# Selective-scan layers: one injection in three on GpSimd, du on VectorE, the B row copied earlier on ScalarE

## The chip, the cores and the metric

The kernel runs on one core of a Trainium2 chip. The metric is the device time of one execution in microseconds (us), from runs of the same program; the profile is of one further execution, with its own time beside it. A core has five engines that the text names as the profile does: PE (TensorE), DVE (VectorE), ACT (ScalarE), POOL (GpSimd) and SP (SyncE, which here only issues DMAs).

## The reference, cut to what matters

Four residual layers work on x of shape (4, 32, 32, 96). Each is `x = x + layer(groupnorm(x))`. Layers 0 and 3 (the "cross" layers) are four-direction selective scans over the 1024 pixels of an image; layer 1 is a small feature layer and layer 2 a scan in one direction. For a cross layer, per image and direction:

```
delta = softplus(dts + bias)              # (192 channels, 1024 pixels)
h[t]  = exp(delta[t]*A)*h[t-1] + delta[t]*u[t]*B[t]     # for each of 16 states
y[t]  = sum over states of h[t]*C[t], plus u[t]*D
```

The four directions' y are summed, normalised over the channels, gated by silu(z) and projected back to 96 channels.

## The kernel before

`cross_scan_layer` is one hand-written program for all engines; every wait is a semaphore wait in the code, and each engine runs its instructions in the written order. A **turn** is one image in one pixel order (rows or columns); there are 4 images x 2 orders = 8 turns in each of the two cross layers, 16 in all. The orders are r = 0 and r = 1. A turn has 16 **groups** of 3 **tiles** (c = 0, 1, 2): 48 tiles of 128 x 1024 float32. The 16 groups are 2 scan directions d times 8 pairs of states p; the three tiles c of a group are three blocks of 64 channels, with two states of each over the 128 partitions.

For each tile the engines do this, with the lines of the kernel before:

- ACT, `turn_of` (L777): decay = exp(delta*A) into one of three SBUF buffers. At c = 1 it first runs `copy_b` (L767): the group's B row, which a DMA has spread over 128 partitions in SBUF (`b_rows`), is copied to one of two PSUM tiles `b_ps`.
- DVE, `inject_tile` (L916): the **injection** du*B, from du in SBUF and the B row in PSUM, into PSUM. Then the **scan** (L931): state = decay*state + injection, along the pixels.
- POOL (L841): the **read**, state*C, from SBUF to SBUF.
- PE (L651): y accumulated in PSUM over the tiles by four matmul instructions.

So the chain of a tile is ACT and DVE, then POOL, then PE. Rings hold it together: a scan waits until the read three tiles back is done (three `state` buffers), a read until the y two tiles back is done (two `read` buffers).

Beside this, the turn does **side work**: it finishes the image before (z, shift, cent, var, out; in r = 0 turns except the first image's) and prepares the next turn's u, B and C, delta and du. The tables FINISH and PREPARE give the tile at which PE issues each half of a side matmul into the only side bank, `side_ps`. ACT takes it at its tile ACT_LAG = 4 later, DVE (for cent, shift, out) at its tile DVE_LAG = 3 later. The next side matmul waits for `side_free`, that the last half has been taken.

The softplus of the next turn is spread over ACT (exp, log, one, less, relu in ACT_SOFTPLUS) and POOL (a subtraction `gap`, L819). Its last step is the side `sum`: three parts by six matmul instructions of 512 columns per half. ACT copies the result to `delta` (L706). Then POOL multiplies du = delta*u, 128 x 1024 at once (L825), and signals `sp_du`, on which SP's `copy_block` waits before it copies delta and du to the layout that the tiles read.

```
PREPARE r=0: ("sum", 0): (34, 35)   ("sum", 1): (39, 40)   ("sum", 2): (42, 43)
PREPARE r=1: ("sum", 0): (28, 29)   ("sum", 1): (31, 32)   ("sum", 2): (36, 37)
```

SP loads the B row of the next group (`load_b`, L528) once the copy of this one is done, since `b_rows` is a single buffer, and the C row (`load_c`, L539); the block copies stand between these loads in the same queue.

## Time and profile before

| what | us |
|---|---|
| median of 3 runs | 3813.66 (3811.82 to 3817.78) |
| the profiled execution's own time | 3815.76 |
| its span, first to last instruction | 3813.9 |
| VectorE busy | 3266.3 (86%) |
| TensorE busy | 2849.4 (75%) |
| GpSimd busy | 2350.1 (62%) |
| ScalarE busy | 2051.3 (54%) |

Busy time of an engine is the time in which one of its instructions ran; 1.9 us of the execution's time lie outside the span. Matmuls are pipelined and their ends are modelled, so PE's busy share says less than the others'. In the timeline a row is a start, a duration, the engine, the line of the kernel, the operation, the tiles written and read, and in brackets the idle time of the engine before it and what ended it.

### The profile page before, as it was taken

How to read it: one execution, taken by the hardware profiler on the slowest of the kernel's cores; microseconds unless marked ns; L12 is line 12 of the kernel's file. 1: busy time of each engine (PE TensorE's matmuls, PEld its weight loads, DVE VectorE, ACT ScalarE, POOL GpSimd, SP SyncE). 2: the span in 40 equal slices, each digit the busy share in tenths (PEclk: the TensorE clock that was granted, in tenths of full speed). 3: DMA queues.
4: the chain of work that ended last, by engine and by line, in shares of the span. 5: the costliest groups of instructions: out<-in, count | busy, mean ns of one | idle time of the engine just before them, and what ended most of it. 6: DMA issues, size and time to landing. Idle time of an engine off the chain costs nothing. (4 is left out here: it accounts for less than half of the span.)

```text
span 3813.9 us, 26717 instructions
## 1 busy us (share of the span) xinstructions
PE 2849.4 (75%) x6084; PEld 648.1 (17%) x6084; DVE 3266.3 (86%) x2104; ACT 2051.3 (54%) x2278; POOL 2350.1 (62%) x1004
## 2 busy tenths in 40 slices
PE   6778777877887788435667677688778887887887
PEld 2111111111111211111111121111111111111111
DVE  1899999999999998585988924999999999999993
ACT  3465555656565655314555425556565556656562
POOL 1677767777776776003656504677676767776773
PEclk9677787878788877767789777677887778788778
DMA  2555546463655554103443405365546555564742
GB/s 57 136 126 139 138 125 143 119 161 97 160 129 133 124 133 117 28 0 84 117 106 85 99 5 122 99 160 133 129 115 142 135 128 126 132 153 109 157 119 62
DMA packets 140377, 436.95 MB, mean 115 GB/s; under 512 B 33429, under 2 KB 34139, under 8 KB 139915
## 3 DMA queue, kind: packets, MB, share of 16 engines
q1 hardware_dynamic: 140234, 435.53, 47.4%
q14 instruction: 112, 0.92, 0.1%
q8 instruction: 31, 0.51, 0.1%
HBM read 307.50 MB, written 6.82 MB: 82 GB/s over the span
## 5 line engine op out<-in xcount | busy, mean ns | idle before, releaser
L841 POOL TENSOR_TENSOR L_read<-L_state,L_c_rows 128x1024 f32<-128x1024 f32 x768 | 1809.0, 2362 | 757.1 <-DVE L_state L931 467.3
L931 DVE TENSOR_TENSOR_SCAN L_state<-L_decay,L_b_ps 128x1024 f32<-128x1024 f32 x768 | 1756.0, 2286 | 29.4 <-DVE L_b_ps L916 2.1
L651 PE MATMUL L_y_ps<-L_read,L_fold 128*64 128x512 f32 x3072 | 1255.0, 913 | 394.8 <-POOL L_read L841 375.5
L916 DVE TENSOR_TENSOR L_b_ps<-L_du,L_b_ps 128x1024 f32<-128x1024 f32 x768 | 937.5, 1221 | 236.0 <-issue 146.4
L777 ACT ACTIVATE L_decay<-L_delta,L_a_neg 128x1024 f32<-128x1024 f32 x768 | 876.4, 1145 | 406.7 <-DVE L_state L931 405.7
L767 ACT COPY L_b_ps<-L_b_rows 128x1024 f32<-128x1024 f32 x256 | 260.1, 1016 | 340.6 <-DVE L_state L931 220.6
L651 PEld LDWEIGHTS L_y_ps<-L_read,L_fold 128*64 128x64 f32 x3072 | 188.0, 161 | 1356.5 <-POOL L_read L841 1017.6
L1461 POOL TENSOR_TENSOR L_read<-L_state,L_c_rows 128x1024 f32<-128x1024 f32 x96 | 237.3, 2477 | 184.3 <-PE L_y_ps L1257 109.5
L1567 DVE TENSOR_TENSOR_SCAN L_state<-L_decay,L_b_ps 128x1024 f32<-128x1024 f32 x96 | 219.5, 2286 | 3.3
L626 PE MATMUL L_side_ps<-L_dbl,L_w_dt 128*128 128x512 f32 x216 | 182.4, 940 | 50.3 <-DVE L_sq_b L902 26.9
L626 PE MATMUL L_side_ps<-g_cm,L_w_u 96*128 (+1 forms) x216 | 179.7, 921 | 41.7 <-ACT L_u L695 40.0
L706 ACT COPY L_delta<-L_side_ps 128x512 f32<-128x512 f32 x108 | 63.0, 583 | 228.7 <-PE L_side_ps L626 228.7
L1545 DVE TENSOR_TENSOR L_b_ps<-L_du,L_b_ps 128x1024 f32<-128x1024 f32 x96 | 117.3, 1222 | 67.2 <-DMA L_du<-L_du_a 41.5
L1257 PE MATMUL L_y_ps<-L_read,L_fold 128*64 128x512 f32 x384 | 125.5, 731 | 57.9 <-POOL L_read L1461 50.3
L1410 ACT ACTIVATE L_decay<-L_delta,L_a_neg 128x1024 f32<-128x1024 f32 x96 | 108.9, 1143 | 67.4 <-DVE L_state L1567 40.6
L626 PE MATMUL L_side_ps<-L_delta,ident 128*128 128x512 f32 x216 | 122.0, 649 | 0.0
L819 POOL TENSOR_TENSOR L_y_b<-L_more,L_y_b 128x1024 f32<-128x1024 f32 x18 | 42.6, 2368 | 128.2 <-ACT L_more L737 128.2
L1439 POOL TENSOR_TENSOR L_l_a<-L_more,L_l_a 128x1024 f32<-128x1024 f32 x4 | 9.4, 2352 | 168.7 <-ACT L_more L1339 168.7
L825 POOL TENSOR_TENSOR L_du<-L_delta,L_u 128x1024 f32<-128x1024 f32 x36 | 85.3, 2369 | 23.9 <-ACT L_delta L706 23.9
L695 ACT COPY L_u<-L_side_ps 128x512 f32<-128x512 f32 x108 | 61.8, 573 | 52.1 <-PE L_side_ps L626 51.7
L626 PE MATMUL L_side_ps<-L_y_a,ident 128*128 128x512 f32 x72 | 52.7, 822 | 41.7 <-ACT L_delta L704 18.5
L658 PE MATMUL L_y_ps<-L_u,L_skip_diag 64*64 64x512 f32 x192 | 81.3, 934 | 0.0
(315 smaller groups left out, 2677.3 us busy)
## 6 DMA issues: line engine op xcount, KB each, us to landing
L_c_rows<-L_bc_dram SPq DMA_DIRECT2D x580, 256.0 KB, 4.0
L_b_rows<-L_bc_dram SPq DMA_DIRECT2D x580, 256.0 KB, 4.2
L_delta<-L_delta SPq DMA_DIRECT2D x204, 256.0 KB, 5.8
L_du<-L_du SPq DMA_DIRECT2D x140, 256.0 KB, 5.8
L_du<-L_u SPq DMA_DIRECT2D x64, 256.0 KB, 6.1
L_bc_dram<-L_dbl SPq DMA_DIRECT2D x40, 128.0 KB, 3.4
L_delta<-L_delta_a SPq DMA_DIRECT2D x16, 256.0 KB, 4.4
L_du<-L_du_a SPq DMA_DIRECT2D x16, 256.0 KB, 5.5
```

Source lines behind the costliest of these rows:

```text
L626: m = nc.tensor.matmul(side_ps[0:rows, :], lhs, rhs, start=(k == 0), stop=(k == len(parts) - 1))
L651: m = nc.tensor.matmul(y_ps[i * BLK:(i + 1) * BLK, c, :], fold[:, :], y_half(t, o, i), start=first, stop=last, skip_group_check=True)
L767: nc.scalar.copy(b_ps[g % 2][:, :], b_rows[:, :]).then_inc(b_ready, 1)
L777: nc.scalar.activation(decay[:, t % DECAYS, :], delta2[:, d * NBLK + c, :], ACT.Exp, scale=a_neg[:, o * 2 + d, c, p:p + 1]).then_inc(decay ...
L841: nc.gpsimd.tensor_tensor(read[:, t % READS, :], state[:, t % STATES, :], c_rows[:, g % 2, :], ALU.mult).then_inc(multiplied, 1)
L916: nc.vector.tensor_tensor(to[:, :], du2[:, d * NBLK + c, :], row[:, :], ALU.mult).then_inc(injected, 1)
L931: nc.vector.tensor_tensor_scan(state[:, t % STATES, way], decay[:, t % DECAYS, way], fed[:, way], 0.0, ALU.mult, ALU.add).then_inc(scanned, 1)
L1257: m = nc.tensor.matmul(y_ps[quarter(i), c, :], fold[:, :], read[:, t % READS, s], start=t < NBLK, stop=t >= NT - NBLK, skip_group_check=True)
L1410: nc.scalar.activation(decay[:, t % DECAYS, :], delta2[:, slot(number, c), :], ACT.Exp, scale=a_neg[:, c, p:p + 1]).then_inc(decay_ready, 1)
L1461: nc.gpsimd.tensor_tensor(read[:, t % READS, :], state[:, t % STATES, :], c_rows[:, p % 2, :], ALU.mult).then_inc(multiplied, 1)
L1545: nc.vector.tensor_tensor(to[:, :], du2[:, slot(number, c), :], row[:, :], ALU.mult).then_inc(injected, 1)
L1567: nc.vector.tensor_tensor_scan(state[:, t % STATES, :], decay[:, t % DECAYS, :], fed[:, :], 0.0, ALU.mult, ALU.add).then_inc(scanned, 1)
```

## The change

In the cross layers only:

- POOL forms the injection of c = 2 (`inject_c`), from du and `b_rows` in SBUF straight into the state buffer of c = 2. The scan of c = 2 reads it there and writes over it. DVE keeps the injections of c = 0 and 1.
- So that this scan still has one operand in PSUM, ACT writes the decay of c = 2 to the PSUM tile `work_ps`. The two `b_ps` become `row_ps` (the B row; the injection of c = 1 is written over it) and `work_ps` (the injection of c = 0, then the decay of c = 2). There are two decay buffers in SBUF in place of three, one per c.
- `b_rows` becomes two buffers; a load waits for both the ACT copy and the POOL injection of two groups back.
- du moves to DVE, per half of 512 columns, straight from `side_ps`, at DVE's tile three after PE's. ACT's copy of the same half to `delta` waits for it.
- ACT's order within a group: at c = 0 only `sum` copies follow the decay; other side and softplus work of that tile comes after the row's copy and the decay of c = 1.

```
@@ POOL
+            def inject_c(number, g):
+                d, last = g // NP, NBLK - 1
+                if g % NP == 0:
+                    pool.wait_ge(du2_in[d * NBLK + last], (number + 1) * PER_BLOCK)
+                pool.wait_ge(b_in[g % 2], (number * (GROUPS // 2) + g // 2 + 1) * 32)
+                pool.wait_ge(multiplied, (number * GROUPS + g) * NBLK + MULT0)
+                nc.gpsimd.tensor_tensor(state[:, last, :], du2[:, d * NBLK + last, :], b_rows[:, g % 2, :],
+                                        ALU.mult).then_inc(injected_c, 1)
...
+                    if t % NBLK == 0:
+                        inject_c(number, g)
                     pool.wait_ge(scanned, number * NT + t + 1 + SCAN0)
...
-                    if t in POOL_SOFTPLUS[turn.r]:
-                        softplus(turn, *POOL_SOFTPLUS[turn.r][t])
+                    if t in POOL_GAP[turn.r]:
+                        gap(turn, POOL_GAP[turn.r][t])
@@ DVE
+                if kind == "sum" and i == 0:
+                    for q in range(2 * j, 2 * j + 2):
+                        dve.wait_ge(du2_in[q], turn.next * PER_BLOCK)
                 dve.wait_ge(side_ready, use + 1)
+                if kind == "sum":
+                    nc.vector.tensor_tensor(du[j][:, s], side_ps[:, :], u[:, j, s], ALU.mult).then_inc(sp_du, 1)
+                    return
...
-                    fed = inject_tile(number, t)
-                    dve.wait_ge(injected, T + 1 + INJECT0)
+                    if c < 2:
+                        by, fed = decay[:, c, :], inject_tile(number, t)
+                    else:
+                        by, fed = work_ps, state[:, c, :]
+                        dve.wait_ge(injected_c, number * GROUPS + g + 1 + READY0)
@@ ACT
                 elif kind == "sum":
+                    if not isinstance(turn, Head):
+                        act.wait_ge(sp_du, 2 * (turn.next * NJ + j) + i + 1 - NJ)
                     ins = nc.scalar.copy(delta[:, j, s], side_ps[:, :])
...
+                    if c == 2:
+                        act.wait_ge(scanned, number * NT + t - 1 + SCAN0)
+                    to = work_ps if c == 2 else decay[:, c, :]
...
+                    if c == 0:
+                        take_sides(turn, t, True)
+                    else:
+                        if c == 1:
+                            take_sides(turn, t - 1, False)
+                            side_work(turn, t - 1)
+                        take_sides(turn, t, True)
+                        take_sides(turn, t, False)
+                        side_work(turn, t)
@@ SP
                 sp.wait_ge(b_ready, G + 1)
+                sp.wait_ge(injected_c, G + 1)
```

What this makes of the engines' orders, at three places of the first turn. POOL's order, before, in the stretch of the softplus (L819 is `gap`, L825 is du, L841 the read):

```order
L841 TENSOR_TENSOR L_read<-L_state,L_c_rows 128x1024 x7
L819 TENSOR_TENSOR L_sq_b<-L_more,L_sq_b 128x1024
L841 TENSOR_TENSOR L_read<-L_state,L_c_rows 128x1024
L825 TENSOR_TENSOR L_du<-L_delta,L_u 128x1024
L841 TENSOR_TENSOR L_read<-L_state,L_c_rows 128x1024 x2
L819 TENSOR_TENSOR L_gate_b<-L_more,L_gate_b 128x1024
L841 TENSOR_TENSOR L_read<-L_state,L_c_rows 128x1024 x2
L825 TENSOR_TENSOR L_du<-L_delta,L_u 128x1024
```

and in the change (L850 is `gap`, L865 `inject_c`, L878 the read):

```order
L865 TENSOR_TENSOR L_state<-L_du,L_b_rows 128x1024
L878 TENSOR_TENSOR L_read<-L_state,L_c_rows 128x1024
L850 TENSOR_TENSOR L_sq_b<-L_more,L_sq_b 128x1024
L878 TENSOR_TENSOR L_read<-L_state,L_c_rows 128x1024 x2
L865 TENSOR_TENSOR L_state<-L_du,L_b_rows 128x1024
L878 TENSOR_TENSOR L_read<-L_state,L_c_rows 128x1024
L850 TENSOR_TENSOR L_gate_b<-L_more,L_gate_b 128x1024
L878 TENSOR_TENSOR L_read<-L_state,L_c_rows 128x1024 x2
```

One injection now stands ahead of every three reads, and the three du of a turn are gone.

DVE's order, before, over tiles 37 to 39 (L916 is the injection, L931 the scan, printed under its instruction's form):

```order
L916 TENSOR_TENSOR L0_b_ps1<-L0_du2,L0_b_ps0 128x1024
L931 SCALAR_TENSOR_TENSOR L0_state<-L0_decay,L0_b_ps1 128x1024
L916 TENSOR_TENSOR L0_b_ps0<-L0_du2,L0_b_ps0 128x1024
L931 SCALAR_TENSOR_TENSOR L0_state<-L0_decay,L0_b_ps0 128x1024
L916 TENSOR_TENSOR L0_b_ps0<-L0_du2,L0_b_ps1 128x1024
```

and in the change (L967 is the injection, L986 the scan, L944 a half of du):

```order
L944 TENSOR_TENSOR L0_du_01<-L0_side_ps,L0_u 128x512
L967 TENSOR_TENSOR L0_row_ps<-L0_du2,L0_row_ps 128x1024
L986 SCALAR_TENSOR_TENSOR L0_state<-L0_decay,L0_row_ps 128x1024
L944 TENSOR_TENSOR L0_du_01<-L0_side_ps,L0_u 128x512
L986 SCALAR_TENSOR_TENSOR L0_state<-L0_work_ps,L0_state 128x1024
L967 TENSOR_TENSOR L0_work_ps<-L0_du2,L0_row_ps 128x1024
```

The third injection is gone; a half of du stands ahead of the work of tiles 37 and 38, and the scan of tile 38 takes its injection from the state buffer.

ACT's order, before, from tile 39 on (L767 is the row's copy, L777 the decay, L706 the copy to delta, L695 that to u, the rest softplus):

```order
L777 ACTIVATE L0_decay<-L0_delta2,L0_a_neg 128x1024
L706 COPY L0_delta<-L0_side_ps 128x512
L737 ACTIVATE L0_more<-L0_more,L0_minus_col 128x1024
L724 ACTIVATE L0_gate_a<-L0_gate_a 128x1024
L767 COPY L0_b_ps1<-L0_b_rows 128x1024
L777 ACTIVATE L0_decay<-L0_delta2,L0_a_neg 128x1024
L695 COPY L0_u<-L0_side_ps 128x512
L729 ACTIVATE L0_gate_b<-L0_gate_a 128x1024
```

and in the change (L779, L810, L713, L700 in the same roles):

```order
L810 ACTIVATE L0_decay<-L0_delta2,L0_a_neg 128x1024
L713 COPY L0_delta<-L0_side_ps 128x512
L779 COPY L0_row_ps<-L0_b_rows 128x1024
L810 ACTIVATE L0_decay<-L0_delta2,L0_a_neg 128x1024
L749 ACTIVATE L0_more<-L0_more,L0_minus_col 128x1024
L736 ACTIVATE L0_gate_a<-L0_gate_a 128x1024
L700 COPY L0_u<-L0_side_ps 128x512
L741 ACTIVATE L0_gate_b<-L0_gate_a 128x1024
```

The row's copy now comes ahead of the two softplus steps of its group's first tile, but still behind the copy to delta.

## Rows read from the trace of the kernel before

**Rows 1.** The page's first part: busy time, share of the span, instructions.

```profile
PE 2849.4 (75%) x6084; PEld 648.1 (17%) x6084; DVE 3266.3 (86%) x2104; ACT 2051.3 (54%) x2278; POOL 2350.1 (62%) x1004
```

**Rows 2.** Groups by cost: line, engine, tiles, count | busy us, mean ns | idle before, releasers.

```profile
L841 POOL TENSOR_TENSOR L_read<-L_state,L_c_rows 128x1024 f32<-128x1024 f32 x768 | 1809.0, 2362 | 757.1 <-DVE L_state L931 467.3
L931 DVE TENSOR_TENSOR_SCAN L_state<-L_decay,L_b_ps 128x1024 f32<-128x1024 f32 x768 | 1756.0, 2286 | 29.4 <-DVE L_b_ps L916 2.1
...
L916 DVE TENSOR_TENSOR L_b_ps<-L_du,L_b_ps 128x1024 f32<-128x1024 f32 x768 | 937.5, 1221 | 236.0 <-issue 146.4
L777 ACT ACTIVATE L_decay<-L_delta,L_a_neg 128x1024 f32<-128x1024 f32 x768 | 876.4, 1145 | 406.7 <-DVE L_state L931 405.7
L767 ACT COPY L_b_ps<-L_b_rows 128x1024 f32<-128x1024 f32 x256 | 260.1, 1016 | 340.6 <-DVE L_state L931 220.6
```

**Rows 3.** DVE's timeline: the first injections of three turns in a row (r = 0, 1, 0).

```profile
455.44 1.23 DVE L916 TENSOR_TENSOR L_b_ps<-L_du,L_b_ps 128x1024 f32<-128x1024 f32 x1 [0.33 <-ACT L_b_ps L767]
...
635.81 1.23 DVE L916 TENSOR_TENSOR L_b_ps<-L_du,L_b_ps 128x1024 f32<-128x1024 f32 x1
...
807.99 1.23 DVE L916 TENSOR_TENSOR L_b_ps<-L_du,L_b_ps 128x1024 f32<-128x1024 f32 x1 [0.98 <-ACT L_b_ps L767]
```

**Rows 4.** DVE's timeline: one plain group, tiles 18 to 20 of an r = 1 turn.

```profile
699.65 1.23 DVE L916 TENSOR_TENSOR L_b_ps<-L_du,L_b_ps 128x1024 f32<-128x1024 f32 x1
700.91 2.29 DVE L931 TENSOR_TENSOR_SCAN L_state<-L_decay,L_b_ps 128x1024 f32<-128x1024 f32 x1
703.23 1.23 DVE L916 TENSOR_TENSOR L_b_ps<-L_du,L_b_ps 128x1024 f32<-128x1024 f32 x1
...
706.70 1.21 DVE L916 TENSOR_TENSOR L_b_ps<-L_du,L_b_ps 128x1024 f32<-128x1024 f32 x1
707.94 2.29 DVE L931 TENSOR_TENSOR_SCAN L_state<-L_decay,L_b_ps 128x1024 f32<-128x1024 f32 x1
```

**Rows 5.** Timelines of ACT and DVE at tile 45 of an r = 0 turn.

```profile
624.06 1.02 ACT L767 COPY L_b_ps<-L_b_rows 128x1024 f32<-128x1024 f32 x1 [5.74 <-DMA L_b_rows<-L_bc_dram]
...
625.20 1.23 DVE L916 TENSOR_TENSOR L_b_ps<-L_du,L_b_ps 128x1024 f32<-128x1024 f32 x1 [5.20 <-ACT L_b_ps L767]
```

**Rows 6.** DVE's timeline: a side half of 512 columns ahead of an injection.

```profile
508.55 0.66 DVE L899 TENSOR_TENSOR x_cm<-x_cm,L_side_ps 96x512 f32 x1
509.13 1.22 DVE L916 TENSOR_TENSOR L_b_ps<-L_du,L_b_ps 128x1024 f32<-128x1024 f32 x1
```

**Rows 7.** POOL's timeline near the end of an r = 1 turn.

```profile
783.03 2.38 POOL L841 TENSOR_TENSOR L_read<-L_state,L_c_rows 128x1024 f32<-128x1024 f32 x1 [2.29 <-PE L_y_ps L651]
...
787.71 11.68 POOL L841 TENSOR_TENSOR L_read<-L_state,L_c_rows 128x1024 f32<-128x1024 f32 x5
```

**Rows 8.** Who waited for whom: us in total, times, longest.

```profile
POOL L_read L841 <- PE L_y_ps L651: 289.3, 141, 7.5
...
ACT L_b_ps L767 <- DMA L_b_rows<-L_bc_dram: 118.0, 32, 6.1
```

**Rows 9.** PE's timeline: sum halves and the y behind them (r = 0), a y in r = 1.

```profile
592.32 1.13 PE L626 MATMUL L_side_ps<-L_y_a,ident 128*128 128x512 f32 x2
...
595.09 1.08 PE L651 MATMUL L_y_ps<-L_read,L_fold 128*64 128x512 f32 x4
...
626.68 2.07 PE L626 MATMUL L_side_ps<-L_gate_a,ident 128*128 128x512 f32 x2 [4.47 <-ACT L_delta L706]
...
631.89 1.94 PE L651 MATMUL L_y_ps<-L_read,L_fold 128*64 128x512 f32 x8
...
785.47 1.92 PE L651 MATMUL L_y_ps<-L_read,L_fold 128*64 128x512 f32 x4 [0.89 <-POOL L_read L841]
```

**Rows 10.** Stretches: us, then busy us of PE, PEld, DVE, ACT, POOL, PEclk, DMA, GB/s.

```profile
635.80:808.00 172.20, 144.06 (x280) 27.02 (x276) 167.04 (x97) 98.61 (x106) 132.13 (x57) 0.78 0.57 136
560.00:636.00 76.00, 55.34 (x128) 15.09 (x130) 68.55 (x42) 49.28 (x56) 57.19 (x26) 0.84 0.53 126
```

**Rows 11.** Layer 2, two lines: count, duration ns min/median/max, first and last start.

```profile
L1515 DVE SCALAR_TENSOR_TENSOR L_conved<-L_padded_a,L_conv_w,L_conved x32: 1257/1285/3273, 1704.9 to 2031.9; 128x1024 f32<-128x1024 f32 x32
...
L1461 POOL TENSOR_TENSOR L_read<-L_state,L_c_rows x96: 2335/2354/3455, 1759.3 to 2196.1; 128x1024 f32<-128x1024 f32 x96
```

More of the change, by code:

```diff
@@ L449, in cross_scan_layer @@
         c_in = [sem(f"c_in{d}") for d in range(2)]
+        b_in = [sem(f"b_in{d}") for d in range(2)]
         PER_BLOCK = 16 * 2
-        MULT0, SCAN0, SUM0, INJECT0 = NBLK + 1, DECAYS, READS, 1
+        MULT0, SCAN0, SUM0, INJECT0, READY0 = NBLK + 1, DECAYS, READS, 1, 2
         class Turn:
@@ L508, in copy_block @@
                 rows = slice(half * BLK, half * BLK + BLK)
-                sp.wait_ge(sp_du, n * NJ + j + 1)
+                if isinstance(n, int) and n == 0:
+                    sp.wait_ge(sp_du, j + 1)
+                else:
+                    sp.wait_ge(delta_ready, n * NJ + j + 1)
                 for side in range(2):
@@ L690, in take @@
                         if j == 0:
-                            act.wait_ge(sp_du, turn.next * NJ)
+                            act.wait_ge(sp_du, turn.next * NJ * 2 - NJ)
                         if j == 2:
@@ L705, in take @@
                 elif kind == "sum":
+                    if not isinstance(turn, Head):
+                        act.wait_ge(sp_du, 2 * (turn.next * NJ + j) + i + 1 - NJ)
                     ins = nc.scalar.copy(delta[:, j, s], side_ps[:, :])
+                    if i == 1:
+                        ins.then_inc(delta_ready, 1)
+                        act.wait_ge(delta_ready, turn.next * NJ + j + 1)
+                        act.sem_inc(side_free, 1)
+                        return
                 elif kind == "z":
@@ L761, in take_y, with copy_b, take_sides, side_work @@
                 act.sem_inc(y_free, 1)
-            def copy_b(G, g):
-                act.wait_ge(b_in, 32 * (G + 1))
+            def copy_b(number, G, g):
+                act.wait_ge(b_in[g % 2], (number * (GROUPS // 2) + g // 2 + 1) * 32)
                 act.wait_ge(scanned, (G - 1) * NBLK + 2 + SCAN0)
-                nc.scalar.copy(b_ps[g % 2][:, :], b_rows[:, :]).then_inc(b_ready, 1)
+                nc.scalar.copy(row_ps[:, :], b_rows[:, g % 2, :]).then_inc(b_ready, 1)
+            def take_sides(turn, t, sums):
+                for at, key, i in turn.sides:
+                    if at == t - ACT_LAG and key[0] in ACT_SIDES and (key[0] == "sum") == sums:
+                        take(turn, key, i)
+            def side_work(turn, t):
+                if turn.finish and t == SILU_AT:
+                    silu(turn)
+                if turn.finish and t == RSTD_AT:
+                    root(turn)
+                for (kind, j), at in ACT_SOFTPLUS[turn.r].items():
+                    if at == t:
+                        softplus(turn, kind, j)
             def turn_of(turn):
@@ L812, in _, with gap @@
         def _(pool):
-            def softplus(turn, kind, j):
+            def gap(turn, j):
                 n = turn.next * NJ + j
-                if kind == "gap":
-                    pool.wait_ge(sp_log, n + 1)
-                    pool.wait_ge(sp_less, n + 1)
-                    l = l_of[j]
-                    nc.gpsimd.tensor_tensor(l[:, :], more[:, :], l[:, :], ALU.subtract).then_inc(sp_gap, 1)
-                else:
-                    wait_side(pool, turn.use(("sum", j), 1))
-                    if not isinstance(turn, Head):
-                        for q in range(2 * j, 2 * j + 2):
-                            pool.wait_ge(du2_in[q], turn.next * PER_BLOCK)
-                    nc.gpsimd.tensor_tensor(du[j], delta[:, j, :], u[:, j, :], ALU.mult).then_inc(sp_du, 1)
+                pool.wait_ge(sp_log, n + 1)
+                pool.wait_ge(sp_less, n + 1)
+                l = l_of[j]
+                nc.gpsimd.tensor_tensor(l[:, :], more[:, :], l[:, :], ALU.subtract).then_inc(sp_gap, 1)
             def add_x(turn):
@@ L844, in turn_of, with form_du @@
                         add_x(turn)
-                    if t in POOL_SOFTPLUS[turn.r]:
-                        softplus(turn, *POOL_SOFTPLUS[turn.r][t])
-            for kind, j in (("gap", 0), ("gap", 1), ("du", 0), ("gap", 2), ("du", 1), ("du", 2)):
-                softplus(Head(), kind, j)
+                    if t in POOL_GAP[turn.r]:
+                        gap(turn, POOL_GAP[turn.r][t])
+            def form_du(j):
+                wait_side(pool, Head().use(("sum", j), 1))
+                nc.gpsimd.tensor_tensor(du[j], delta[:, j, :], u[:, j, :], ALU.mult).then_inc(sp_du, 1)
+            gap(Head(), 0)
+            gap(Head(), 1)
+            form_du(0)
+            gap(Head(), 2)
+            form_du(1)
+            form_du(2)
             over_turns(pool, turn_of)
@@ L930, in turn_of @@
                     way = slice(None, None, 1 if d == 0 else -1)
[L931 to L932 removed]
+                    nc.vector.tensor_tensor_scan(state[:, c, way], by[:, way], fed[:, way], 0.0, ALU.mult,
+                                                 ALU.add).then_inc(scanned, 1)
             over_turns(dve, turn_of)
```

61 lines of the change are left out of this document (26 added, 35 removed).

## The prediction

> **What bounds the kernel now.** I read the page's first part, then the groups by cost, then DVE's timeline at the turns' edges, and last the waits. The first part [rows 1] shows DVE busy for 86% of the span and POOL for 62%; that is an average over all layers. The groups [rows 2] show what DVE does: 768 scans of 2.286 us and 768 injections of 1.221 us in the two cross layers. Neither waits for another engine for long; the 236.0 us ahead of the injections are mostly two waits for a layer to start. POOL sat idle for 757.1 us between its reads. The turn edges [rows 3] give the length of a turn: 635.81 - 455.44 = 180.4 us for r = 0 and 807.99 - 635.81 = 172.2 us for r = 1. A plain group [rows 4] takes 707.94 + 2.29 - 699.65 = 10.58 us, so 16 of them 169.3. DVE therefore sets the pace: the r = 1 turn is 98% plain groups, and the r = 0 turn adds eight side halves and a stall of 5.20 us where a B row came late [rows 5].
>
> **The change, part by part.** Per turn, against those two lengths.
>
> *DVE loses an injection per group.* In the plain group the piece from the first injection to the second is 703.23 - 699.65 = 3.58 us, and to the third 3.47 [rows 4]. The third tile keeps its scan: 2.29, less the 0.08 by which an operation without a wait starts ahead of the end of the one before it, and 0.03 until the next injection: 2.24. New group: 3.47 + 3.47 + 2.24, plus 0.1 for the wait that stays at c = 0, 9.28 us. Sixteen make 148.5.
>
> *DVE gains six halves of du per turn.* A side half of this size takes 0.66 us and moves the next injection by 509.13 - 508.55 = 0.58 [rows 6]: 3.5 us. DVE's own floor is 152 us for r = 1. For r = 0 eight halves of 0.58 are there already: 156.6 us.
>
> *POOL gains an injection per group and loses three du per turn.* Five reads in a row took 11.68 us [rows 7], 2.34 each; a lone one takes 2.36 [rows 2]. I price the injection like a read, the same form from SBUF to SBUF. It waits for POOL's own read of c = 2 to end; the trace has no such wait on POOL, and I take 0.1 us, like DVE's wait on its own scan (3.58 - 3.47, [rows 4]). Bounds: nothing, and 0.2 us, twice that (1.6 us per turn either way). Group: 3 x 2.34 + 2.36 + 0.1 = 9.48 us; 16 make 151.7. Three gaps (7.1 us) make 158.8 for r = 1; the finished image's addition to x makes 161.1 for r = 0. **POOL's floor is above DVE's**: POOL becomes the pace-setter, by a little. From 172.2 and 180.4 this alone would save 13.4 and 19.3 us.
>
> *The late B row goes.* With two `b_rows` buffers a load has a whole group more. ACT waited 118.0 us for this row in all [rows 8]; what reached DVE, such as the 5.20 us [rows 5], is inside the turn lengths, so the floors above already count it as gone. SP passes the block copies in the same order as before, and `delta_ready` rises at about the place where `sp_du` did.
>
> *ACT's copy and decay.* DVE can no longer run on the next B row before it is copied: the copy can only start after the scan of c = 1 and has the scan of c = 2 to hide in: 1.016 against 2.286 us [rows 2]. The decay of c = 2 must fit between the end of the scan of c = 0 and that of c = 1, 1.145 us in 3.47. Both are covered unless side work stands ahead of them. ACT needs 3 x 1.145 + 1.016 = 4.45 us of each 9.48, which leaves 5.0 for side work. In the softplus stretch ACT was busy for 49.28 of 76 us [rows 10]; at the new pace it would be near three quarters. Cost: 0 to 2 us per turn, I take 1 in r = 0 and 0.5 in r = 1.
>
> *The new wait loop at du.* This is the part that costs. PE's second half of a sum waits for `side_free`, thus for ACT's copy of the first half, and that now waits for DVE's du, which stands behind the scan two tiles after. Behind that, on DVE, wait the injection and scan; on ACT, the B row's copy or the next decay. Round the loop: du 0.66, copy about 0.58 (an ACT copy of half the size of a row's, at 1.016), sum half, semaphores 0.3. At full clock a half took 595.09 - 592.32 = 2.77 us, at the low level 631.89 - 626.68 = 5.21 [rows 9]. That is 4.3 or 6.75 us where a tile now has 9.48/3 = 3.16: 1.2 or 3.6 us lost per pair of halves. The granted clock in this stretch was 0.84 [rows 10], so about two thirds of the time at 2.4 GHz and one third at 1.2: 2.0 us per pair, three pairs, **6 us per turn**. Bounds: 0, if PE's queue is so far behind that DVE and ACT have always been there, and 26 us, six halves at the low level each missing a tile by 5.21 + 1.94 - 3.16 = 4.0 and POOL unable to absorb any.
>
> *PE behind POOL.* POOL waited 289.3 us for y [rows 8], mostly free as POOL had slack. In r = 1 a y takes 1.92 us [rows 9], and PE was busy for 144.06 of 172.20 us [rows 10]; at 159 it would be over 90%. I count it inside the 6 us for the sums, since the worst place is the same one [rows 7].
>
> *Where two engines share memory.* Layer 2 shows a price: there DVE's operation with two SBUF inputs took 1.26 us alone and up to 3.27 beside POOL's read, which itself went from 2.35 to as much as 3.46 [rows 11]. In the cross layers no injection or scan shows it: their means are those of undisturbed ones [rows 2], and each has one operand in PSUM. The moved scan keeps one in `work_ps`, du has one in `side_ps`. I price contention at 0.
>
> *Twice the work on the slower engine.* The injection takes 2.36 us where it took 1.22 [rows 2]. It fits because POOL had 757.1 us idle and because its loop is short: read of c = 2, injection, scan, next read are 2.36 + 0.1 + 2.36 + 2.29 + 0.1 = 7.2 of the 9.48 us of a group. The Trainium skill, "GPSIMD Engine Reference", Engine selection, speaks against such a move: elementwise work belongs on VectorE, as GpSimd is about twice as slow with two inputs. The rows give the same ratio, 1.93. Were the two engines' work one chain, as the rule by itself would have it, each group would be 2.36 - 1.22 = 1.14 us longer; by the rows the two run side by side, and the sum goes by these.
>
> **The sum.** r = 0: 161.1 + 6 + 1 = 168.1; r = 1: 158.8 + 6 + 0.5 = 165.3, less about 1 where DVE's stall gives POOL its gaps for nothing: 164.3. Savings: six r = 0 turns of later images 180.4 - 168.1 = 12.3 each, 74; the first image's two, which finish nothing and which I put at the same 12.3, 25; eight r = 1 turns 7.9 each, 63. Together 162 us. The profiled execution took 3815.8 us (2.1 above the median): 3654, and from the median 3652. I say **3650 us**.
>
> **Rivals.**
>
> *POOL paces cleanly.* The du loop is hidden. Saving 8 x 19.3 + 8 x 13.4 = 262 us: 3552. For it: POOL's lag lets DVE run ahead, and ACT had idle time. Against: six halves per turn through one bank. Chance 0.18.
>
> *PE paces the r = 1 turns and the softplus stretch.* With y at 1.92 us and PE 84% busy in r = 1 the turn may not shrink: r = 1 stays at 170 (2 gained), and r = 0 gains half of its 19.3: 16 + 77 = 93, 3720. For it: the 289.3 us. Against: these waits lie in a few places. Chance 0.17.
>
> *The du loop costs more than the injections gave (slower).* Mechanism and place: DVE, in order, stands before tiles 37, 38 and so on until PE's half is there. It decides from a stall of 16.4/6 = 2.7 us per half over POOL's floor (mean of 19.3 and 13.4). At the upper bound of 4.0 with ACT's blocked row copy behind it (1.016 more, not hidden) it is 5.0 a half: 30 - 16.4 = 14 us lost per turn, 3814 + 218 = 4032; at 3.5 a half, 3890. For it: PE is at the low level for a third of this stretch. Against: the next half at full clock misses by 1.2 only, and POOL's lag of some two reads absorbs part. Chance 0.08.
>
> *Contention, or the moved injection on the chain.* If the scan of c = 2, now reading and writing the state buffer beside a busy POOL, were stretched by the 2.0 us of layer 2, a group would be 11.3 us against 10.58: 16 x 16 x 0.7 = 180 us slower, 3994. If the injection stood on the chain of every group, 256 x 1.14 = 292 us slower, 4106; it does so from the point where the loop of 7.2 us exceeds the group's 9.48. The rows speak against both. Chance 0.02 each. That the change does nothing is excluded by the orders shown.
>
> **How the numbers follow.** The forecast has 0.53; its own range, with the bounds of the unequal terms, is 3590 to 3700. The range of 8 in 10 takes in the clean rival and the PE rival, with the lowest tenth and the slower cases left out: 3555 to 3775. A measurement of this kernel can tell 0.2%, 7.6 us, from no change. Faster: 0.18 + 0.53 + 0.15 of the PE rival's 0.17, so 0.86; within 0.2%: the other 0.02; slower: 0.08 + 0.02 + 0.02 = 0.12.
>
> **What would show it.** Scans of 2.286 us and POOL operations near 2.36, both unstretched: no contention. POOL over 90% busy in the cross turns, and DVE's idle time ended by POOL's injection or by du's side matmul: the forecast. Turns of 164 to 169 us. It is wrong if the idle time ahead of L944 is above 16 us per turn (the slower rival), or if turns of r = 1 stay above 170 with POOL waiting on y (the PE rival).

## The result and the profile after

The changed kernel took 3832.47 us (median of 4 runs, 3831.84 to 3836.0) where the kernel before took 3812.74 on the same chip (4 runs, 3807.25 to 3817.78). The ratio is 1.0057, with a 95% interval of 1.0043 to 1.0071: **slower by 0.57%**. The prediction said 3650 us, in a range that ends at 3775, so both the sign and the range were wrong.

The profiled execution has a span of 3830.0 us, 16.1 above that of before, and a granted clock of 0.785 as a mean, where before had 0.779. The clock therefore does not explain the loss. The page's first part and five of its groups, to be read beside [rows 1, 2]:

```profile
PE 2818.0 (74%) x6084; PEld 639.3 (17%) x6084; DVE 3004.5 (78%) x1944; ACT 2044.4 (53%) x2278; POOL 2826.0 (74%) x1212
...
L878 POOL TENSOR_TENSOR L_read<-L_state,L_c_rows 128x1024 f32<-128x1024 f32 x768 | 1799.7, 2360 | 244.7 <-PE L_y_ps L656 210.0
...
L986 DVE TENSOR_TENSOR_SCAN L_state<-L_work_ps,L_state 128x1024 f32<-128x1024 f32 x256 | 583.6, 2280 | 169.1 <-POOL L_state L865 160.7
L810 ACT ACTIVATE L_work_ps<-L_delta,L_a_neg 128x1024 f32<-128x1024 f32 x256 | 286.1, 1118 | 648.7 <-DVE L_state L986 648.6
L865 POOL TENSOR_TENSOR L_state<-L_du,L_b_rows 128x1024 f32<-128x1024 f32 x256 | 605.5, 2365 | 25.7 <-POOL L_read L878 3.7
...
L713 ACT COPY L_delta<-L_side_ps 128x512 f32<-128x512 f32 x108 | 62.9, 583 | 165.5 <-DVE L_du L944 113.3
```

The work moved as the diff says. VectorE's busy time fell by 261.8 us (3266.3 to 3004.5), and POOL's rose by 475.9. The prices were right too: an injection on POOL takes 2.365 us, a read 2.360, and a scan 2.28 to 2.29, as in [rows 2]. The plain group also came out as forecast. This is VectorE's timeline over the second group of an r = 1 turn:

```profile
637.79 1.23 DVE L967 TENSOR_TENSOR L_work_ps<-L_du,L_row_ps 128x1024 f32<-128x1024 f32 x1
639.14 2.29 DVE L986 TENSOR_TENSOR_SCAN L_state<-L_decay,L_work_ps 128x1024 f32<-128x1024 f32 x1
...
644.79 2.27 DVE L986 TENSOR_TENSOR_SCAN L_state<-L_work_ps,L_state 128x1024 f32<-128x1024 f32 x1
647.09 1.23 DVE L967 TENSOR_TENSOR L_work_ps<-L_du,L_row_ps 128x1024 f32<-128x1024 f32 x1
```

It is 647.09 - 637.79 = 9.30 us long, against 10.58 before [rows 4] and the 9.28 that the prediction worked out. VectorE saved its 262 us and still the span grew by 16.1, so it stood idle for 278 us more. The waits tell where (the columns are us in total, times, longest us):

```profile
POOL L_read L878 <- PE L_y_ps L656: 210.0, 134, 5.0
DVE L_state L986 <- POOL L_state L865: 160.7, 72, 5.9
...
PEld L_side_ps L631 <- ACT L_u L700: 118.1, 46, 6.1
PEld L_side_ps L631 <- ACT L_delta L709: 116.5, 58, 3.9
ACT L_delta L713 <- DVE L_du L944: 113.3, 48, 4.3
...
DVE L_du L944 <- PE L_side_ps L631: 72.5, 40, 4.4
...
DVE x_cm L951 <- PE L_side_ps L631: 70.3, 10, 23.1
...
DVE L_work_ps L967 <- ACT L_row_ps L779: 32.9, 25, 3.3
...
DVE L_u L944 <- PE L_side_ps L631: 23.3, 24, 2.3
```

The largest new one is VectorE waiting 160.7 us for POOL's injection, in 72 of 256 groups. The du halves cost it 72.5 + 23.3 = 95.8 us (the third part's du lies in the buffer `u`), which is 6.0 us per turn.

The length of a turn shows which turns lost. It is worked out from VectorE's timeline, from the start of a turn's first injection to the end of its last scan; "edges" is the sum of the 14 gaps between one turn and the next within a layer. The forecast counts a turn from start to start, so its numbers hold an edge (0.8 us before); its entry for the first image is 177.3 less the 12.3 that it gave every r = 0 turn. The lower lines are runs of the next section.

| kernel | r = 0, first image (mean of 2) | r = 0, later images (mean of 6) | r = 1 (mean of 8) | edges, sum |
|---|---|---|---|---|
| before | 177.3 | 179.5 | 172.0 | 10.9 |
| forecast | 165.0 | 168.1 | 164.3 | |
| after | 170.0 | **187.2** | 168.7 | 17.5 |
| ScalarE's order put back (e5) | 166.9 | 180.7 | 167.1 | 13.7 |
| and du back on POOL (e13) | 165.0 | 176.7 | 170.2 | 52.4 |
| only du back on POOL (e3) | 169.8 | 183.4 | 171.8 | 51.8 |
| before, with du on VectorE alone (e14) | 179.5 | 182.7 | 175.5 | 4.5 |
| before, with ScalarE's new order alone (e12) | 181.2 | 188.8 | 174.3 | 9.9 |

The first image's turns and r = 1 gained 7 and 3 us; the six r = 0 turns that also finish an image lost 8 each. The worst place is in one of those, layer 0. First PE's timeline, then ScalarE's, POOL's and VectorE's of the same stretch:

```profile
837.84 1.08 PE L656 MATMUL L_y_ps<-L_read,L_fold 128*64 128x512 f32 x4
842.87 2.07 PE L631 MATMUL L_side_ps<-g_cm,L_w_u 96*128 x2 [3.94 <-ACT L_u L700]
844.87 1.98 PE L656 MATMUL L_y_ps<-L_read,L_fold 128*64 128x512 f32 x4
...
840.25 1.02 ACT L779 COPY L_row_ps<-L_b_rows 128x1024 f32<-128x1024 f32 x1 [0.69 <-DMA L_b_rows<-L_bc_dram]
841.20 1.15 ACT L810 ACTIVATE L_decay<-L_delta,L_a_neg 128x1024 f32<-128x1024 f32 x1
842.25 0.56 ACT L700 COPY L_u<-L_side_ps 128x512 f32<-128x512 f32 x1
...
847.00 2.35 POOL L878 TENSOR_TENSOR L_read<-L_state,L_c_rows 128x1024 f32<-128x1024 f32 x1 [2.74 <-PE L_y_ps L656]
849.43 2.34 POOL L865 TENSOR_TENSOR L_state<-L_du,L_b_rows 128x1024 f32<-128x1024 f32 x1
...
851.90 2.29 DVE L986 TENSOR_TENSOR_SCAN L_state<-L_work_ps,L_state 128x1024 f32<-128x1024 f32 x1 [2.73 <-POOL L_state L865]
861.48 0.68 DVE L951 TENSOR_TENSOR x_cm<-x_cm,L_side_ps 96x512 f32 x1 [7.29 <-PE L_side_ps L631]
```

Read it from the top. PE is done with its y at 838.9 and wants the side bank, but ScalarE empties the bank only at 842.25, because in its new order the row's copy (which itself waits 0.69 us for its row) and the next decay stand ahead of that take. With the order put back (e5), the same take starts 1.04 us after the start of the decay ahead of it; here it is 842.25 - 838.42 = 3.83 us. PE idles for 3.94 us, with the next y queued behind the side matmul. POOL's read waits 2.74 us for that y to free its buffer, POOL's injection follows the read, and VectorE's scan waits 2.73 us for the injection. Its shift half (L951) then waits 7.29 us for PE, which by now runs at 2.07 us a pair instead of 1.1.

### The profile page after: what moved, and what is told of

The parts are those of the page before. It is cut to its first block and busy times, and to the rows that moved or that the text cites. A ratio compares the mean times of both kernels' runs of the same rounds, so it can differ in the third digit from the quotient of the medians.

```text
span 3830.0 us, 27831 instructions
## 1 busy us (share of the span) xinstructions
PE 2818.0 (74%) x6084; PEld 639.3 (17%) x6084; DVE 3004.5 (78%) x1944; ACT 2044.4 (53%) x2278; POOL 2826.0 (74%) x1212
## 5 line engine op out<-in xcount | busy, mean ns | idle before, releaser
L878 POOL TENSOR_TENSOR L_read<-L_state,L_c_rows 128x1024 f32<-128x1024 f32 x768 | 1799.7, 2360 | 244.7 <-PE L_y_ps L656 210.0
L986 DVE TENSOR_TENSOR_SCAN L_state<-L_work_ps,L_state 128x1024 f32<-128x1024 f32 x256 | 583.6, 2280 | 169.1 <-POOL L_state L865 160.7
L810 ACT ACTIVATE L_work_ps<-L_delta,L_a_neg 128x1024 f32<-128x1024 f32 x256 | 286.1, 1118 | 648.7 <-DVE L_state L986 648.6
L865 POOL TENSOR_TENSOR L_state<-L_du,L_b_rows 128x1024 f32<-128x1024 f32 x256 | 605.5, 2365 | 25.7 <-POOL L_read L878 3.7
L986 DVE TENSOR_TENSOR_SCAN L_state<-L_decay,L_row_ps 128x1024 f32<-128x1024 f32 x256 | 585.5, 2287 | 32.2 <-POOL L_read L878 23.9
L986 DVE TENSOR_TENSOR_SCAN L_state<-L_decay,L_work_ps 128x1024 f32<-128x1024 f32 x256 | 585.3, 2286 | 29.9 <-DVE L_work_ps L967 6.8
L810 ACT ACTIVATE L_decay<-L_delta,L_a_neg 128x1024 f32<-128x1024 f32 x512 | 584.5, 1142 | 15.0 <-DVE L_state L986 8.3
L967 DVE TENSOR_TENSOR L_work_ps<-L_du,L_row_ps 128x1024 f32<-128x1024 f32 x256 | 314.3, 1228 | 188.2 <-issue 144.5
L779 ACT COPY L_row_ps<-L_b_rows 128x1024 f32<-128x1024 f32 x256 | 260.1, 1016 | 241.5 <-DVE L_state L986 140.3
L967 DVE TENSOR_TENSOR L_row_ps<-L_du,L_row_ps 128x1024 f32<-128x1024 f32 x256 | 309.6, 1209 | 0.0
L1622 DVE TENSOR_TENSOR_SCAN L_state<-L_decay,L_b_ps 128x1024 f32<-128x1024 f32 x96 | 219.5, 2286 | 3.3
L1600 DVE TENSOR_TENSOR L_b_ps<-L_du,L_b_ps 128x1024 f32<-128x1024 f32 x96 | 117.3, 1222 | 70.3 <-DMA L_du<-L_du_a 41.7
L713 ACT COPY L_delta<-L_side_ps 128x512 f32<-128x512 f32 x108 | 62.9, 583 | 165.5 <-DVE L_du L944 113.3
L1465 ACT ACTIVATE L_decay<-L_delta,L_a_neg 128x1024 f32<-128x1024 f32 x96 | 108.9, 1143 | 66.6 <-DVE L_state L1622 40.4
L850 POOL TENSOR_TENSOR L_y_b<-L_more,L_y_b 128x1024 f32<-128x1024 f32 x18 | 42.5, 2362 | 128.1 <-ACT L_more L749 128.1
```

Of the source, the lines that this page charges most:

```text
L779: nc.scalar.copy(row_ps[:, :], b_rows[:, g % 2, :]).then_inc(b_ready, 1)
L810: nc.scalar.activation(to[:, :], delta2[:, d * NBLK + c, :], ACT.Exp, scale=a_neg[:, o * 2 + d, c, p:p + 1]).then_inc(decay_ready, 1)
L865: nc.gpsimd.tensor_tensor(state[:, last, :], du2[:, d * NBLK + last, :], b_rows[:, g % 2, :], ALU.mult).then_inc(injected_c, 1)
L878: nc.gpsimd.tensor_tensor(read[:, t % READS, :], state[:, t % STATES, :], c_rows[:, g % 2, :], ALU.mult).then_inc(multiplied, 1)
L967: nc.vector.tensor_tensor(to[:, :], du2[:, d * NBLK + c, :], row_ps[:, :], ALU.mult).then_inc(injected, 1)
L986: nc.vector.tensor_tensor_scan(state[:, c, way], by[:, way], fed[:, way], 0.0, ALU.mult, ALU.add).then_inc(scanned, 1)
```

## The experiments

The expectations use letters. **A**: the cost is ScalarE's new order, which takes side halves later; a number behind it tells forms of this theory apart. **P**: PE's y work is too slow for a POOL that has become busy. **D**: the du loop through the one side bank, the prediction's slower rival. All ratios are to the kernel before.

**e1 and e2, half of the y work.** P: in the inner groups each y matmul takes half of its columns, in the changed kernel (e1) and in the kernel before (e2).

```
...
+                        if not first and not last:
+                            to, src = to[:, 0:HALF // 2], (src[:, 0:HALF // 2] if o == 0 else src[:, 0:H // 4, :])
```

> The changed kernel, but the y matmuls of all groups but a turn's edge tiles take half of their columns, so that PE has about half the y work (this leaves part of the sum over states out of the output). Theory P (PE's y comes late, POOL's reads wait for it, POOL's injection behind them, and DVE's scan of c = 2 behind that): the 160 us that the scans of c = 2 wait for POOL fall below 60, the time falls by 100 us or more, to about 3720 or less. Theory A (ACT takes side results too late because its decay of c = 2 waits for a scan of the same group, and PE stands at side_free): the scans still wait over 110 us, time above 3780. Theory D (the du loop): the wait ahead of du stays near 70 us, time above 3780.

> The kernel before with the same half of the y work left out. DVE paced it and absorbed the waits on y: all theories expect little, P 3770 to 3810 (only the few stalls of DVE behind reads go), so that the gap between e1 and e2 is over 50 us in favour of e1. A and D expect e1 and e2 within 30 us of each other.

e1 took 3800.94 us (0.9972, 0.9958 to 0.9986), 31 below the change; e2 3812.74 (1.0003, 0.9993 to 1.0013). The kernel before shows no difference. The changed one does, but far less than P asked for, and as A expected: VectorE's wait for the injection fell from 160.7 to 111.3 us, while that ahead of the du halves rose from 95.8 to 130.8. The test is blunter than meant, since with fewer columns the mean granted clock fell from 0.785 to 0.702 in e1, and from 0.779 to 0.676 in e2; so neither run shows what less PE work at an unchanged clock would give.

**e3, du back on POOL.** D. POOL forms the three du of a turn as before, and ScalarE's copy to `delta` waits no longer.

```
-                    nc.vector.tensor_tensor(du[j][:, s], side_ps[:, :], u[:, j, s], ALU.mult).then_inc(sp_du, 1)
...
+                    if t in POOL_DU[turn.r]:
+                        form_du(turn, POOL_DU[turn.r][t])
```

> The changed kernel with du back on POOL at its old places, ACT's copy free of it. Theory D: 60 us or more faster than the change (its 72 us of waits ahead of du and 56 us of du itself go), about 3750. Theory P: POOL and PE pace; POOL gets three more operations of 2.36 us per turn (113 us in all), so no faster than 20 us below the change, rather 0 to 60 us slower, 3830 to 3890. Theory A: like the change within 25 us.

3872.54 us (1.0164, 1.0142 to 1.0186): slower than the change by 40, where D expected 60 or more faster and P up to 60 slower. D falls: du on VectorE is worth 40 us to this kernel.

**e4, takes one tile earlier.** A. ScalarE empties the side bank one tile sooner (all sides but the sums), in the new order.

```
-                    if at == t - ACT_LAG and key[0] in ACT_SIDES and (key[0] == "sum") == sums:
+                    if at == t - (ACT_LAG if sums else ACT_LAG - 1) and key[0] in ACT_SIDES and (key[0] == "sum") == sums:
```

> The changed kernel with ACT taking every side result but the sums one tile earlier (lag 3 in place of 4). Theory A: PE's waits for side_free fall and the time by 40 us or more, below 3795. Theory P and D: within 15 us of the change, 3817 to 3847.

3774.03 us (0.9907, 0.9885 to 0.9928), 58 below the change. PE's waits for the bank fell as A expected: those that ScalarE's takes of u and dt ended went from 118.1 and 116.5 us to 41.7 and 81.3.

**e5, ScalarE's order as before.** A, by undoing the third part of the change and nothing else.

```
-                    if c == 0:
-                        take_sides(turn, t, True)
-                    else:
-                        if c == 1:
-                            take_sides(turn, t - 1, False)
-                            side_work(turn, t - 1)
-                        take_sides(turn, t, True)
-                        take_sides(turn, t, False)
-                        side_work(turn, t)
+                    take_sides(turn, t, True)
+                    take_sides(turn, t, False)
+                    side_work(turn, t)
```

> The changed kernel with ACT's order within a group as before: side and softplus work of c = 0 right behind its decay, ahead of the row's copy. Theory A1 (ACT is late because the change puts the side takes of c = 0 behind the row's copy and the next decay): 30 us or more faster than the change, under 3803. Theory A2 (it is late because the decay of c = 2 now waits for a scan of the same group, whatever the order): not faster; the row's copy comes later, DVE's waits for it rise from 43 us to over 100, time 3835 to 3900.

3772.07 us (0.9901, 0.9877 to 0.9924): **60 below the change and 1% below the kernel before**. A1 holds; A2 was right that the waits for the row's copy rise over 100 us, and wrong on the time. Waits of e5:

```profile
POOL L_read L872 <- PE L_y_ps L656: 183.3, 120, 4.9
...
DVE L_work_ps L961 <- ACT L_row_ps L779: 121.2, 91, 3.8
...
PEld L_side_ps L631 <- ACT L_delta L709: 97.4, 48, 4.8
...
PEld L_side_ps L631 <- ACT L_u L700: 91.0, 56, 2.5
...
DVE L_state L980 <- POOL L_state L859: 79.5, 69, 4.1
```

The reordering did what it was written to do: VectorE's waits for the row's copy are 121.2 us here and 32.9 with it, 88 less. But with it the waits for the injection are 160.7 and not 79.5, and those ahead of the du halves 95.8 and not 72.4 (the rest at shift and at reads): the 88 us were paid for more than once. The mean granted clock moved with the order, 0.798 in e5 and 0.785 in the change; how much of the 60 us came by way of the clock, no run separates.

**e6, a third read buffer.** P. To find room, `b_rows` went back to one buffer.

```
-DECAYS, STATES, READS = 3, 3, 2
+DECAYS, STATES, READS = 3, 3, 3
...
-        b_rows = sb("b_rows", [128, 2, L])
+        b_rows = sb("b_rows", [128, 1, L])
```

> The changed kernel with three read buffers in place of two, so that a read waits for the y three tiles back; the memory comes from b_rows, single again. Theory P: POOL's 210 us of waits on y fall under 100, the scans' 160 us on POOL under 80, time 40 us or more below the change, under 3793. Theory A: PE stands still all the same behind side_free and the third buffer fills; time within 20 us of the change, or slower by the late B rows, up to 3880.

4059.11 us (1.0654, 1.0634 to 1.0673). The waits show why this says little on P:

```profile
ACT L_row_ps L779 <- DMA L_b_rows<-L_bc_dram: 673.3, 206, 7.7
```

With one buffer the next B row can't be loaded before POOL's injection has read the last one, and ScalarE waited for it in 206 of 256 groups. So the second `b_rows` buffer is no refinement: the change depends on it. A third read buffer beside it wasn't tried.

**e7 and e8, which takes count.** e4's step for only those halves that PE issues at c = 2 (e7), or at c = 1 (e8).

```
+                    if at == t - (ACT_LAG if sums or not (at % NBLK == 2) else ACT_LAG - 1) and key[0] in ACT_SIDES and (key[0] == "sum") == sums:
```

> Lag 3 only for those side halves that PE issues at c = 2: ACT takes them behind its decay of c = 2, in place of behind the next group's copy and decay. Theory A: the larger part of the 58 us that lag 3 gave, 30 to 50 us below the change (3782 to 3802), with DVE's waits for the row's copy near 100 us. If the position does not matter: within 12 us of the change.

> Lag 3 only for the side halves that PE issues at c = 1: ACT takes them behind its decay of c = 1, in place of behind that of c = 2. Theory A: a smaller part, 10 to 30 us below the change (3802 to 3822), DVE's waits for the row's copy staying near 43 us. If the position does not matter: within 12 us of the change.

e7: 3806.04 us (0.9985, 0.9971 to 0.9999), 26 below the change and so a little short of what A expected. e8: 3818.44 (1.0031, 1.0016 to 1.0047), 14 below. With the lag of 4, a half issued at c = 2 is taken at c = 0, the ones that the new order defers; they bring the larger share, and the c = 1 halves some of the rest.

**e9, takes or softplus.** At c = 0 the takes follow the decay at once, as before; the softplus and other long work stay behind the row's copy, as in the change.

```
...
+                    if c == 1:
+                        side_work(turn, t - 1)
+                    take_sides(turn, t, True)
+                    take_sides(turn, t, False)
+                    if c > 0:
                         side_work(turn, t)
```

> The changed kernel, where at c = 0 ACT takes the side results right behind the decay, but does the softplus and other long side work behind the row's copy and the decay of c = 1. Theory A1 (what counts is when side_ps is set free; the copy then waits only for short takes): 10 to 40 us below e5 (3732 to 3762), DVE's waits for the row's copy well under the 121 us of e5. If the softplus steps themselves must be early (they feed POOL's gap and so the sums): between e5 and the change, 3775 to 3815.

3777.95 us (0.9900, 0.9876 to 0.9925), as e5, and not the 10 to 40 us below it that A1 expected. VectorE's waits for the row's copy did fall, from 121.2 us in e5 to 75.5, but those for the injection rose from 79.5 to 102.6. The deferred takes are the whole cost; deferring softplus work neither costs nor gains any time that shows.

**e10 and e11, both remedies.** e5 with e4's lag (e10), and e9 with it (e11).

> ACT's order within a group as before and lag 3 for all sides but the sums. Theory A1: both do the same thing, set side_ps free earlier; together little more than each: 3755 to 3775. If they are two independent delays, the gains add: about 3715. If ACT then stands before PE's result with the row's copy behind it: above 3780, with DVE's waits for the copy over 150 us.

> e9 with lag 3 as well. Theory A1: about as e9, within 15 us. If ACT then blocks before the copy: 20 us or more above e9.

3799.07 us (0.9957, 0.9941 to 0.9974) and 3810.79 (0.9991, 0.9977 to 1.0005). Each remedy alone gains about 60 over the change, together 33 and 22. A1 missed, and the last case of each expectation came true. Waits of e10, to be read beside those of e5:

```profile
DVE L_work_ps L961 <- ACT L_row_ps L779: 247.8, 143, 6.4
...
ACT L_u L700 <- PE L_side_ps L631: 125.8, 66, 4.8
...
DVE L_state L980 <- POOL L_state L859: 19.5, 23, 1.4
```

POOL's waits for y fall from 183.3 us to 139.1, and VectorE's for the injection from 79.5 to 19.5. But ScalarE now stands before PE's side half, 125.8 us at the u halves alone where e5 has 63.1, with the row's copy in its queue behind the take, and VectorE's waits for that copy double from 121.2 to 247.8 us. In e11 they are 191.9, against 75.5 in e9. So a take can come too early as well as too late.

**e12, the new order in the kernel before.** Does the reordering cost only because the change shortened the rings?

> The kernel before with one part of the change alone: ACT's new order within a group (row's copy and decay of c = 1 ahead of the side and softplus work of c = 0). Theory A1: the later takes hold PE up here too, but three tiles of elasticity between DVE, POOL and PE take most of it: 0 to 20 us slower than before, 3810 to 3832. If the order costs by itself, whatever the rings: 40 to 60 us slower, 3850 to 3872.

3900.27 us (1.0233, 1.0215 to 1.0251): 88 slower, more than either form of the theory expected. It costs by itself, without any of the rest. Its waits, beside [rows 8]:

```profile
POOL L_read L856 <- PE L_y_ps L651: 428.3, 197, 7.0
...
PEld L_side_ps L626 <- ACT L_u L695: 183.2, 60, 7.0
PEld L_side_ps L626 <- ACT L_delta L704: 181.3, 78, 6.5
```

and the last two in the kernel before:

```profile
PEld L_side_ps L626 <- ACT L_u L695: 119.0, 57, 4.1
PEld L_side_ps L626 <- ACT L_delta L704: 104.5, 55, 3.3
```

PE waits longer for the bank to be emptied, and POOL's wait for y goes from 289.3 to 428.3 us. On VectorE, which paced this kernel, the waits for the row's copy go from 69.4 to 102.6 us, those at the shift half from 46.7 to 72.4, and those for POOL's reads from 1.1 to 27.4: 85 us together. The mean granted clock was 0.765, before 0.779.

**e13 and e14, the two other parts alone.** The moved injection with du on POOL and ScalarE's order as before (e13: e3's and e5's edits together), and du on VectorE in the kernel before (e14: the hunks of the diff that move du).

> The change with du back on POOL (three of 2.4 us a turn) and ScalarE's side work in the order of the kernel before: the moved injection, the work_ps decay and the second b_rows buffer alone. If the three parts add up (reordering of ScalarE +60, from the run that undid it; du on VectorE -40, from the run that put it back), then 3772 + 40 = 3812: no gain by the injection without du. Theory A (side takes held up are the cost, and the injection's saving is real): 3800 to 3815. Rival (du on VectorE gives its 40 only because ScalarE's order had slowed the sums): below 3790.

> The kernel before with one part of the change: the du halves on VectorE, straight from the side bank, with the copy to delta behind them; the injections, rings and ScalarE's order stay. VectorE gets six halves of 0.58 us a turn more, 16 x 3.5 = 56 us, and POOL loses work that it had idle time for. If VectorE is the bound of that kernel: 3860 to 3880. Rival (du taken from POOL shortens the softplus chain and the wait for y, as it did on the changed kernel): 3770 to 3813.

e13: 3804.88 us (0.9996, 0.9976 to 1.0016), no change that can be told. e14: 3863.43 (1.0136, 1.0115 to 1.0157), slower by 53. e13 lies where theory A put it, and e14 where it was to be if VectorE bounds that kernel. Together (e5) they are 38 us faster than before. Neither part pays alone, and the sum of the parts has the wrong sign.

The table of turns says what each lends the other. In e14 VectorE is the bound and has 58 us more to do (3324.4 us busy against 3266.3), and turns are 2 to 3.5 us longer. In e13 the turns are shorter than before by 12.3, 2.8 and 1.8 us, but 41 of what they gain is lost between turns: the edges sum to 52.4 us. Timelines of e13 at such an edge, POOL's, SP's, ScalarE's and VectorE's (SP's rows are DMA issues):

```profile
614.01 7.00 POOL L871 TENSOR_TENSOR L_read<-L_state,L_c_rows 128x1024 f32<-128x1024 f32 x3
...
625.72 2.33 POOL L849 TENSOR_TENSOR L_u<-L_delta,L_u 128x1024 f32<-128x1024 f32 x1
...
621.03 1.10 SPq L542 DMA_DIRECT2D L_c_rows<-L_bc_dram  x2
622.30 2.39 SPq L531 DMA_DIRECT2D L_b_rows<-L_bc_dram  x4
...
629.15 1.02 ACT L770 COPY L_row_ps<-L_b_rows 128x1024 f32<-128x1024 f32 x1 [5.55 <-DMA L_b_rows<-L_bc_dram]
...
630.29 1.23 DVE L951 TENSOR_TENSOR L_work_ps<-L_du,L_row_ps 128x1024 f32<-128x1024 f32 x1 [4.44 <-ACT L_row_ps L770]
```

At the end of a turn SP loads the next turn's first C row and, behind it, its first B row. The C row waits for POOL's reads of the last group but one, since it goes into their buffer. These end at 614.01 + 7.00 = 621.01, SP issues the C row at 621.03 and the B row at 622.30, and ScalarE can copy it only at 629.15: it waits 5.55 us and VectorE 4.44. The last du, at 625.72, comes after both loads and holds neither. What decides is how late POOL's reads are. On the mean of the 14 edges the last scan of a turn ends 4.9 us after that read where du is on POOL (e13 and e3), and 8.1 us after it in e5, where POOL has three operations fewer per turn; at this edge VectorE's first injection starts 630.29 - 621.01 = 9.3 us after it. So with du on VectorE most of the edge goes (13.7 us in e5).

## Why the prediction was wrong

The prediction gave a slower kernel a chance of 0.12, by the du loop, by contention or by the injection on the chain. None of the three is what happened. Term by term:

- **VectorE's new group, 9.28 us**: right, 9.30 measured.
- **The injection's price on POOL, 2.36 us, and no contention**: right. It is 2.365 us beside reads of 2.360, with scans of 2.280 to 2.287; the stretch of layer 2 [rows 11] did not appear with one operand in PSUM. The Trainium skill, "GPSIMD Engine Reference", Engine selection, would keep elementwise work off GpSimd; its ratio of about two is here 2.365 / 1.22 = 1.94 [rows 2], and e13 bears the rule out so far as the move alone gained nothing. With du taken off GpSimd in exchange (e5) the kernel still gained 1%.
- **The du loop, 6 us per turn**: the wait itself was right (95.8 us over 16 turns is 6.0 ahead of L944; the slower rival asked for over 16). In its working, the 0.3 us for semaphores was too much: in the changed kernel the steps from the end of one operation of the loop to the start of the next, PE to VectorE to ScalarE to PE, took 0.04, 0.03 and 0.05 us (medians), 0.12 together. Its upper bound, six times 4.0, is 24 us and not 26. The net effect had the wrong sign: du on VectorE gained 40 us (e3 against the change), of which 34 at the turns' edges (51.8 to 17.5), which the prediction did not look at. "SP passes the block copies in the same order as before" was true, but the row loads in that queue wait for POOL's reads, and a full POOL with du on it is late with these.
- **"ACT's copy and decay", 0 to 2 us, 1 in r = 0 and 0.5 in r = 1: this is the step that failed and gave the sign.** The prediction asked whether the copy and decay that were moved ahead would still be hidden. They are. It did not ask who waits for what was moved behind them. By the turns of after and e5 the new order costs 187.2 - 180.7 = 6.5 us in a later r = 0 turn, 3.1 in a first one and 1.6 in r = 1; over 16 turns and their edges 62, and 60 by the runs. That is more than the 20 us by which the change is slower. In the kernel before it costs 88.
- **"PE behind POOL", counted inside the 6 us**: this step failed too. Before, a late y was taken up by POOL's idle time. Now the injection is queued behind the read that waits for that y, so VectorE feels it: 160.7 us in the changed kernel, and 13.8 in each later r = 0 turn, where the prediction had POOL only 161.1 - 156.6 = 4.5 us slower than VectorE. With the order put back it is 6.9.
- **What the forecast lacks with the order put back.** In e5 r = 1 (167.1) and the first image's turns (166.9) are within 3 us of the forecast, but the later r = 0 turns stay at 180.7 against 168.1: 12.6 us six times, 76 us. VectorE idles 23.0 us in such a turn (mean of the six), where the prediction had 168.1 us over a VectorE floor of 156.6, thus 11.5. The largest part is again the term "ACT's copy and decay": 9.8 us for the row's copy, where 1 was put. The injection has 6.9 of it, the du halves 4.3 (put at 6), the shift half 1.6. Followed back along ScalarE, 5.8 of the 9.8 us lead to a take that waits for PE's side half, with the row's copy queued behind it, as in e10. That a faster PE would give these back is argued from the waits and not tested.

"PE behind POOL" was named only for r = 1 and the softplus, where the plain groups do not feel it. The window of the plain group above, in the changed kernel (us; busy us of PE, PEld, DVE, ACT and POOL; granted clock, DMA share, GB/s):

```profile
637.80:647.10 9.30, 8.95 (x20) 1.47 (x20) 9.11 (x6) 4.29 (x4) 9.22 (x5) 0.50 0.60 136
```

It kept its 9.30 us at a granted clock of 0.50, the lower level, as it has no side half.

That PE's speed decides in a stretch of the finishing turns can be seen within one kernel. Windows of e13, with the same columns, over the second and third groups (by VectorE's injections) of four later r = 0 turns:

```profile
456.41:481.00 24.59, 23.19 (x46) 4.23 (x46) 18.33 (x10) 12.58 (x15) 16.55 (x8) 0.66 0.53 123
814.10:838.80 24.70, 23.51 (x46) 4.33 (x46) 18.33 (x11) 12.39 (x15) 16.54 (x8) 0.64 0.53 122
1170.94:1190.16 19.22, 17.82 (x46) 3.43 (x46) 18.33 (x10) 12.79 (x15) 16.57 (x8) 0.85 0.69 156
2693.29:2712.51 19.22, 17.83 (x46) 3.44 (x46) 18.33 (x10) 12.79 (x15) 16.57 (x8) 0.86 0.70 153
```

The same piece of program takes 19.2 us at a mean granted clock of 0.85 and 24.6 at 0.65, and PE is busy for over nine tenths of either. VectorE's and POOL's work is the same in all four. A timeline of PE in the first and third:

```profile
465.93 1.98 PE L654 MATMUL L_y_ps<-L_read,L_fold 128*64 128x512 f32 x4
467.84 1.97 PE L661 MATMUL L_y_ps<-L_u,L_skip_diag 64*64 64x512 f32 x4
469.74 2.08 PE L629 MATMUL L_side_ps<-g_cm,L_w_z 96*128 x2
...
1181.68 1.08 PE L654 MATMUL L_y_ps<-L_read,L_fold 128*64 128x512 f32 x4
1182.69 1.08 PE L661 MATMUL L_y_ps<-L_u,L_skip_diag 64*64 64x512 f32 x4
```

At the lower level one tile's side half, y and skip sum to 2.08 + 1.98 + 1.97 = 6.0 us, where VectorE and POOL need 3.1 per tile. So the idea of the PE rival was right for a stretch of the finishing turns that it did not name; these two groups make 5.4 us of a turn. Its price of 3720 (93 us saved) is nearer to e5 than the forecast is, but it too had left out the order.

What stays open: how much of the 76 us a second side bank, or less PE work at an unchanged clock, would give back. Neither was tried.

## What to carry to other kernels

When an operation is moved ahead on an in-order engine, price what it was moved past: here a take of 0.58 us, the only thing that frees a single bank, had PE, POOL and VectorE behind it, and deferring it cost 60 us of a change that otherwise gained 40. An idle engine's idle time can be a buffer against another engine's jitter, so work moved there makes its waits everybody's. Test a change of several parts by its parts: here two that don't pay alone pay together, and the third undid both.

## What was not expected of the hardware

With half of the y work left out, PE's granted clock was lower: its mean went from 0.785 to 0.702 in the changed kernel, where PE was busy for 2491.4 us in place of 2818.0, and from 0.779 to 0.676 in the kernel before, with 2531.6 in place of 2849.4. What the smaller matmuls would have saved at an unchanged clock was not measured. And a VectorE scan in place, reading and writing the state buffer with its decay in PSUM, ran at 2.280 us beside a POOL that was busy for 155.49 of the 169.50 us of an r = 1 turn, no slower than with its injection in PSUM (2.286).
